# A fused attention and FP4 feed-forward kernel: rounding factors on ScalarE, scale bounds on GpSimd, joined maxima, maxima rows in two transfers, and the last batch's norms by two tiles

## What is computed

```
q_lat = einsum((x @ W_dq.T @ W_uq.T) per head, k_eff);  c_kv = x @ W_dkv.T
attn  = softmax(causal(q_lat @ c_kv.T / sqrt(hs)));     y = (attn @ c_kv) @ v_eff
x  = layernorm(x + y)
fp4(v): scale = max(max|v| over 16 / 6, 1e-12); round v/scale to {0,.5,1,1.5,2,3,4,6}; times scale
h  = silu(fp4(x) @ fp4(w_gate).T) * (fp4(x) @ fp4(w_up).T)
x  = layernorm(x + fp4(h) @ fp4(w_down).T)
```

## Time and profile before

| | |
|---|---|
| runs | 689.79, 690.15, 693.05 us; median 690.15 |
| the profiled execution | 691.02 us, its span 689.1 us |
| instructions | 15253 |
| busy, share of the span | TensorE 78%, VectorE 76%, ScalarE 60%, GpSimd 48% |
| mean granted TensorE clock | 0.912 of full |
| stages | start-up and first maxima to about 72 us; bodies of the four batches to 215, 350, 485 and 622 us; the end from 622 us |

### The profile page before, as it was taken

The page is one execution under the profiler, slowest core; times in us unless marked ns, Lnnn a source line. Parts: engine busy times, 40 slices in busy tenths (PEclk is TensorE's granted clock), DMA queues, the critical chain, the costliest instruction groups (busy, mean ns, idle before and its releaser), DMA issues.

```text
span 689.1 us, 15253 instructions
## 1 busy us (share of the span) xinstructions
PE 538.4 (78%) x5866; PEld 249.4 (36%) x5866; DVE 526.9 (76%) x920; ACT 411.3 (60%) x601; POOL 332.1 (48%) x488
## 2 busy tenths in 40 slices
PE   4356798779889899989798899898688988894523
PEld 2122343333333343434334435353233335242413
DVE  0359777768989889888888889889598894838681
ACT  2300567567777777766677777666567766674230
POOL 4440014101246766563767765537556464537262
PEclk9755699989999999999999999999999997897675
DMA  4285102922030076020130580101300000000000
GB/s 111 53 227 148 33 3 59 210 56 56 2 102 17 3 169 156 2 56 18 47 87 3 130 187 9 48 11 34 88 1 6 1 3 2 2 18 15 0 16 15
DMA packets 34797, 37.97 MB, mean 55 GB/s; under 512 B 6966, under 2 KB 20342, under 8 KB 34726
## 3 DMA queue, kind: packets, MB, share of 16 engines
q1 hardware_dynamic: 33814, 36.46, 21.9%
q10 hardware_dynamic: 912, 0.54, 0.3%
HBM read 19.64 MB, written 16.78 MB: 53 GB/s over the span
## 4 chain that ended last, share of the span: by engine, by line
PE 42%; DVE 30%; issue 8%; POOL 7%; ACT 7%; DMA 3%; SPq 2%; POOLq 0%; ACTq 0%; DVEq 0%
DVE top L924 18%; PE yt_ps L647 13%; PE ring L609 6%; PE ring L626 5%; PE misc L569 4%; PE misc L584 3%; ACT probs L804 3%; PE misc L540 2%; PE ring L596 2%; PE misc L555 1%; PE ring L569 1%; PE misc L575 1%; POOL rstd L1270 1%; DVE h_amax L1023 1%; SPq L448 1%
## 5 line engine op out<-in xcount | busy, mean ns | idle before, releaser
L924 DVE TENSOR_REDUCE top<-ring 128x2 f32<-128x1024 f32 (+3 forms) x384 | 349.2, 948 | 62.5 <-PE ring L609 31.8
L804 ACT ACTIVATE probs<-ring 128x1024 f32<-128x1024 f32 x288 | 292.8, 1026 | 111.0 <-PE ring L596 63.1
L647 PE MATMUL yt_ps<-probs,v_op 128*32 128x512 f32 (+3 forms) x1536 | 159.6, 503 | 0.4 <-ACT probs L804 0.4
L609 PE MATMUL ring<-k_op,q_op 56*128 56x512 f16 (+3 forms) x768 | 125.1, 348 | 33.0 <-DMA k_op<-scratch_k 18.1
L626 PE MATMUL ring<-q_op,k_op 59*128 59x512 bf16 (+3 forms) x768 | 120.9, 338 | 27.2 <-DVE top L924 18.8
L609 PEld LDWEIGHTS ring<-k_op,q_op 56*128 56x128 bf16 x768 | 37.9, 95 | 136.5 <-issue 105.0
L1328 POOL TENSOR_TENSOR r<-r,yq 128x128 f32<-128x128 f32 x32 | 15.0, 469 | 120.7 <-DVE yq L962 120.7
L626 PEld LDWEIGHTS ring<-q_op,k_op 59*128 59x128 f16 x768 | 37.2, 93 | 94.1 <-issue 50.1
L596 PE MATMUL ring<-ident,mask_s 64*128 64x64 bf16 x1024 | 57.6, 194 | 0.0
L596 PEld LDWEIGHTS ring<-ident,mask_s 64*128 64x128 bf16 x1024 | 46.1, 99 | 16.7 <-issue 2.4
L596 PEld LDWEIGHTS ring<-ident,mask_t 64*128 64x128 bf16 x1024 | 45.2, 97 | 15.3 <-issue 2.0
(11 more groups left out here) (183 smaller groups left out, 755.7 us busy)
## 6 DMA issues: line engine op xcount, KB each, us to landing
q_op<-scratch_q SPq DMA_DIRECT2D x32, 224.0 KB
k_op<-scratch_k SPq DMA_DIRECT2D x32, 224.0 KB
scratch_k<-k_part SPq DMA_DIRECT2D x32, 192.0 KB, 3.3
scratch_q<-q_part SPq DMA_DIRECT2D x32, 128.0 KB, 3.2
scratch_q<-q_part SPq DMA_DIRECT2D x16, 192.0 KB, 3.4
xp<-in_L_attn_x_dram SPq DMA_DIRECT2D x4, 512.0 KB, 4.4
r<-in_L_attn_x_dram SPq DMA_DIRECT2D x8, 256.0 KB, 2.9
out_dram<-z SPq DMA_DIRECT2D x8, 256.0 KB, 2.3
```

Source lines behind the costliest of these rows:

```text
L609: last = nc.tensor.matmul(ring[slot][:, e, at:at + n], q_op[lo:lo + ROWS, pair, i * P:(i + 1) * P], k_op[lo:lo + ROWS, pair, kc * CHUNK:kc ...
L647: last = nc.tensor.matmul(yt_ps[32 * q:32 * (q + 1), lo:CHUNK], v_op[:, j, 4 * a + q, :], probs[:, place[tile] % P_RING, q % 2, at:at + CH ...
L804: nc.scalar.activation(probs[:, n % P_RING, :, :], ring[(2 * n + 1) % 3][:, :, :], ACT.Exp, scale=SCALE).then_inc(t_exp.sem, 1)
L924: last = nc.vector.tensor_reduce(top[:, kc, :, p, i], ring[slot][:, :, at:at + w], AX.X, ALU.max)
```

## The change

1. *Maxima rows*: `top_parts` is laid out by row half and part, and `max_rows_in` issues two transfers of three rows each instead of six of one. SyncE, TensorE and ScalarE count two per unit.
2. *Joined maxima*: where a step has the same query tile for both head pairs (two of 18 steps), one reduction of 128x1024 elements into 128x4 replaces two of 128x512 into 128x2.
3. *Factors*: in batches 0 to 2 VectorE only masks the exponent; ScalarE makes the factor by two activations in place, `Relu(e - 1)` and `Copy(ROUND * v + ROUND)`, at new events `hmagic` and `xmagic`. `neg_one` is the bias tile, with one memset more. For the last batch VectorE makes the factor as before, at these events.
4. *Scale bounds*: in batches 0 to 2 `h_wide` is on GpSimd (new event `hwide`); the reciprocal waits for it.
5. *Last batch by two tiles*: statistics, norm, FP4 chain and transposes of x, the down sums, second norm and stores go in four parts of two tiles (k = 0 to 3) instead of two halves of four. Half 1's two parts are transposed through `yt_ps` (k = 2) and `misc` (k = 3); so are the down products. A down part waits for each tile's own copy, and for the sum of the part before it in its bank.
6. *Tile 7 of the last batch* is rounded on VectorE (`ENDING = 7`) instead of on GpSimd.
7. *Tables*: the steps of nearly all events change by 0 to 4, in the end by more; two weighings a unit move by one step each.

```diff
-    W_STEP = [4, 5, 5, 6, 10, 11, 12, 15, 16, 17, 17, 18]
+    W_STEP = [3, 5, 6, 6, 10, 11, 12, 15, 16, 17, 18, 18]
+    def part_of(b, k):
+        return (2, k // 2, slice(2 * k, 2 * k + 2)) if b == B - 1 else (PER, k, slice(PER * k, PER * (k + 1)))
 FFN:
-        "amax": [9, 17, 24, 30, 35, 40, 49, 52], "hinv": [9, 17, 24, 30, 35, 40, 49, 52],
-        "hexp": [11, 21, 26, 33, 39, 41, 51, 53], "hround": [11, 23, 27, 35, 41, 43, 52, 55], "ht": [16, 26, 29, 40, 45, 49, 58, 60],
+        "amax": [10, 15, 24, 31, 35, 41, 49, 52], "hwide": [10, 17, 25, 32, 39, 41, 49, 52],
+        "hexp": [11, 21, 26, 34, 43, 43, 50, 54], "hmagic": [12, 21, 27, 36, 44, 44, 51, 55],
+        "hround": [13, 21, 27, 36, 44, 45, 52, 55], "ht": [16, 26, 31, 40, 47, 49, 58, 62],
 TAIL tables:
-        "gate": [63, 67, 69, 75, 80, 83, 86, 90], "ht": [71, 74, 78, 80, 87, 90, 97, 97],
-        "x1t": [61, 80], "down": [86, 86, 103, 103], "lnrstd": [54, 77], "lnnorm": [55, 77], "xamax": [55, 79],
-        "amax": [67, 70, 74, 78, 82, 87, 89, 95], "hexp": [69, 72, 74, 78, 84, 87, 91, 95],
+        "gate": [64, 66, 69, 74, 81, 81, 85, 87], "ht": [73, 75, 78, 79, 90, 96, 100, 100],
+        "x1t": [63, 63, 79, 79], "down": [86, 86, 101, 101], "lnrstd": [54, 54, 76, 76], "lnnorm": [54, 54, 78, 78], "xamax": [54, 54, 79, 79],
+        "amax": [67, 70, 74, 76, 83, 84, 90, 92], "hexp": [67, 72, 74, 77, 83, 86, 90, 92],
 max_rows_in:
-                for s in range(PARTS):
-                    for e in range(2):
-                        row, m = HALF * e + ROWS + s, MX * s + PAIRS * NT * e
-                        sp.dma_start(q_op[row:row + 1, ...], top_t[m:m + PAIRS * NT, :]).then_inc(mrow_in.sem, 16)
+                for e in range(2):
+                    row, m = HALF * e + ROWS, PARTS * PAIRS * NT * e
+                    sp.dma_start(q_op[row:row + PARTS, ...], top_t[m:m + PARTS * PAIRS * NT, :]).then_inc(mrow_in.sem, 16)
 misc_job:
-                if place in last_job and not (kind == "down" and k % 2):
+                if place in last_job and not (kind == "down" and k % 2 and b < B - 1):
-                    pe.wait_ge(ht_cp.sem, ht_cp.at(b, PER * (c + 1) - 1))
+                    if b < B - 1:
+                        pe.wait_ge(ht_cp.sem, ht_cp.at(b, PER * (c + 1) - 1))
                     for n in range(half * PER // 2, (half + 1) * PER // 2):
+                        if b == B - 1:
+                            pe.wait_ge(ht_cp.sem, ht_cp.at(b, PER * c + n))
 ScalarE:
+            def factor(tile, ready, less, done, b, k):
+                act.wait_ge(ready.sem, ready.at(b, k))
+                nc.scalar.activation(tile, tile, ACT.Relu, bias=neg_one[:, :]).then_inc(less.sem, 1)
+                act.wait_ge(less.sem, less.at(b, k))
+                nc.scalar.activation(tile, tile, ACT.Copy, scale=ROUND, bias=ROUND).then_inc(done.sem, 1)
 maximum:
+                first, kc, p, at, w = S_LIST[s][0]
+                if [piece[0] for piece in S_LIST[s]] == [first, first]:
+                    both = ring[slot][:, :, 0:PAIRS * w].rearrange("q e (p n) -> q e p n", p=PAIRS)
+                    nc.vector.tensor_reduce(top[:, kc, :, :, first], both, AX.X, ALU.max).then_inc(s_max.sem, 1)
+                    return
 h_exponent (x_exponent alike):
-                dve.wait_ge(he_v.sem, he_v.at(b, t))
-                nc.vector.tensor_scalar(hc[:, n, :, :], hc[:, n, :, :], 1.0, ROUND, ALU.max, ALU.mult).then_inc(hc_v.sem, 1)
 GpSimd:
+            def h_bound(b, t):
+                n = t % 2
+                pool.wait_ge(ha_v.sem, ha_v.at(b, t))
+                nc.gpsimd.tensor_scalar(h_wide[:, n, :], h_amax[:, n, :], DOWN / 6.0, DOWN * 1e-12, ALU.mult, ALU.max).then_inc(hw_p.sem, 1)
 VectorE, last batch:
+            def end_h_round(t):
+                n, sh = t % 2, [P, FB, BLOCK]
+                dve.wait_ge(end_hc.sem, end_hc.at(0, t))
+                nc.vector.tensor_tensor(hx[:, n, :, :], hx[:, n, :, :], hc[:, n, :, :], ALU.add).then_inc(end_hu.sem, 1)
+                dve.wait_ge(end_hu.sem, end_hu.at(0, t) - ENDING)
+                nc.vector.tensor_tensor(hx[:, n, :, :], hx[:, n, :, :], hc[:, n, :, :], ALU.subtract).then_inc(end_hr.sem, 1)
+                dve.wait_ge(hs_p.sem, hs_p.at(B - 1, t))
+                dve.wait_ge(end_hr.sem, end_hr.at(0, t) - ENDING)
+                nc.vector.tensor_tensor(hx[:, n, :, :], hx[:, n, :, :], h_sc[:, n, :].unsqueeze(2).to_broadcast(sh), ALU.mult).then_inc(end_hq.sem, 1)
+            def end_sum(k):
+                dve.wait_ge(end_dn.sem, end_dn.at(0, k))
+                nc.vector.tensor_tensor(z[:, c, h, :], to[...][:, h, :], x1[:, m, :], ALU.add).then_inc(end_z.sem, 1)
```

277 lines of the change are left out of this document (171 added, 106 removed).

## The result

| | before | after |
|---|---|---|
| median of the runs | 690.15 us | 687.56 us (686.5 to 690.5) |
| ratio to before | | 0.9958, interval 0.9939 to 0.9977 |
| profiled execution | 691.0 us, span 689.1 | 687.9 us, span 686.0 |

The change takes 0.4% off, about 3 us. The forecast was 675.0 us with a range of 666 to 687: the direction was right, the size was five times too large, and the time lies outside the range.

A forecast was written before the change was run, and what follows sets the result against it. TensorE was taken to lead with VectorE close behind, and a chain after the last body. Rows 7.0, joined maxima 0.7, bodies 3.9, order 1.0 and end 2.5 made 15.1 us off 691.0, 675.9; median 675.0, range 666 to 687.

The forecast's parts named there:

- At 30% on the chain that is 2.4 us: Full bodies: 8.2 us of factors and bounds taken off VectorE, at its 30% of the chain, win 2.4 us a body.
- The trade in the bodies: Factors to ScalarE, bounds to GpSimd: net 1.3 us won in each of three bodies, 3.9 us in all.
- The rival in which ScalarE's waits take what VectorE gives: Full bodies: the moved work gains nothing, so 679 us instead of 675.0; chance 0.22.
- Rows: Maxima rows in two transfers instead of six: they land sooner and shorten four holes in TensorE, 7.0 us won.
- the first and third holes: TensorE's holes of 6.13 us before 140.51 and 4.30 us before 493.19: 1.7 and 2.7 us won by earlier rows.
- Joined maxima: 32 pairs of 512-element reductions become one of 1024 each, 2.2 to 4.8 us less on VectorE: 0.7 us won.
- Order in the last body: TensorE waits 2.6 us before transposing the last batch's first xq; transposes two steps later win 1.0 us.
- The end: Last batch's norms by two tiles: three stretches of -1.3, -1.4 and +0.2 us, 2.5 us won in all.
- The new stall at down.1: Second stretch of the end: down.1 waits for VectorE's sum of down.0, leaving VectorE idle 2.7 us.
- The third stretch: From the last down product on: half-size sum and norm save 1.1 us, a second power costs 1.3, net +0.2.
- ScalarE as the bound: Rival in the bodies: ScalarE's thirty pairs ahead of exps make the kernel slower, likely 700 us; chance 0.08.
- an even trade, no gain at the end and late rows together: Three rivals at once, in bodies, end and maxima rows: 687.4 us, within 0.5% of no change; chance 0.08.

The follow-up runs named there:

- the base: The changed kernel with factors and scale bounds of batches 0 to 2 back on VectorE, new tables kept: 680.46 us, measured again 679.60 us.

## Why the prediction was wrong, and where it was right

**What bounds the kernel: right in its rows, wrong in its use.** TensorE leads, and the limit stated was that lightening VectorE can return 6 us a body at most. The step that failed is the next one: "At 30% on the chain that is 2.4 us". It was multiplied into every microsecond taken off VectorE, and in the changed kernel TensorE's waits for `top` in a body are 6.4 us where they were 5.8 and "under 3" was forecast, with 9.6 us of VectorE's work gone. They are the same 6.4 in the base, with 5.7 us more of that work. Whether the share holds for relief alone stayed open: 25% was found, with an error twice as large as itself. With the work put elsewhere there was nothing left of it. The relief itself was mis-sized too: 8.2 us a body were forecast, and the move took 5.7 to 5.9, since at the new steps a factor takes 0.36 us and not 0.538.

**The trade in the bodies (forecast -3.9 us; it costs 7 to 9, by the ratios of the change and of the two measurements with all work back).** ScalarE's durations were right: 0.587 and 0.497 us for a tile's pair, 0.721 and 0.630 for a half batch's, against 1.09 and about 1.3. ScalarE's load by itself is worth 2.5 us, near the forecast 3.3, though not clear of nothing. What was missed is the new wait. The prediction named it, with the exp queued behind it, and then dismissed it: "The new tables put them one or two steps apart, about 2 to 4 us, which covers it mostly." The tables do not say that. Of the eight tile factors six stand one step behind their exponent, one two steps, and one at the same step; of the half batches' factors one is a step behind and the other at the same step (15); and all eight bounds stand at the step of the reciprocal that waits for them, for which VectorE stood 9.3 us. For the tiles the waits stayed small all the same (3.8 us in four of 24). For the half batches they did not: 14.3 us of idle in six instructions, 2.4 each, since VectorE was itself behind when it reached the exponent. The first half's three waits, one step apart, are as long as the second half's with none (2.4 to 2.7 and 2.1 to 2.6 us). So the count of steps alone does not tell; what tells is when VectorE gets to the exponent, and that was not looked up in the trace of before. One step more was enough: it gives back 7 us over the kernel, though the profile shows only 2.8 of them in a full body that keeps them. The rival in which ScalarE's waits take what VectorE gives was right in kind and too mild; its even trade was exceeded. The mark set for a wrong step ("over 8 us" of TensorE's wait for exps) was too coarse: the loss came about with 3.7 us. How the rest of it reached TensorE was not traced further.

On the page's rule weighed there, that relu and mul belong on VectorE (the Trainium skill, "ScalarE: Activation LUTs", "Rules for kernel authors"): it was right in sign here, as the change stands. The 9 us given as its price by engine time were mis-worked: they set ScalarE's 33.9 us against VectorE's 24.6 with the bounds among them, which went to GpSimd; for the factors alone, at the rows' durations, it is 33.9 - 15.6 = 18.3 us. That the move did cost 7 to 9 us is a coincidence: with the longest waits gone it was 1.6, which is not clear of nothing.

**Rows (forecast 7.0, measured 4.0, 2.6 to 5.5).** The issues cost 1.51 / 2 = 0.75 us, inside the bounds. The mis-sized terms are the first and third holes, 1.7 and 2.7 forecast, 0.6 and 1.0 found with the rows alone. At the first the prediction had the rows land as soon as the earlier traffic let them; their packets did move then, by 138.0, and TensorE started another 1.3 us later.

**Joined maxima (0.7).** Its duration was right, its worth nothing measurable.

**Order in the last body (1.0).** TensorE's wait there is 2.91 us instead of 2.59, so the term is wrong by its sign. Over the body's last 18 steps the changed kernel takes 34.1 us against 30.7, at a mean granted clock of 0.85 instead of 0.94; that the body is 2.3 us shorter as a whole comes from its first 54 steps. The reason was in the prediction (VectorE's chain is late), but transposes two steps later do not help when `yq` is what is late.

**The end (forecast -2.5, found -3.9).** To the first transposes of the second half, from the last exp: 22.6 us before, 20.4 after, -2.1 against -1.3. From there to the last down products 31.2 and 31.1, -0.1 against -1.4. The new stall at down.1 is there as forecast, 3.02 us against 2.7:

```profile
657.90 0.42 DVE L1151 TENSOR_TENSOR z<-misc,x 128x256 f32<-128x256 f32 x1 [3.02 <-PE misc L599]
```

What cancelled the rest is that TensorE still waits 5.60 and 4.75 us for GpSimd's rounding ahead of the last tiles' transposes. Tile 7's rounding took 0.53 us an instruction, the low value of the earlier trace rows, since GpSimd had just ended tile 6; the exclusive lock of the Trainium skill's "SBUF — State Buffer" ("SBUF: two separate sides"), weighed with 3.7 us, did not come to bear on these three, though the three ahead of them took 1.19, 0.95 and 0.83 us under GpSimd's work. The third stretch took 11.3 us instead of 13.0, -1.7 against +0.2. Its error is a missed overlap: part 2 is summed while TensorE does part 3, and the power of two elements took 0.73 us instead of 1.05.

**The range.** The case that came about was a costly trade of the bodies together with rows at 4 and a good end. The list has an even trade at 679 and ScalarE as the bound at 700, and no trade between them. It does have a place for the number: 0.08 for an even trade, no gain at the end and late rows together, 687.4. That this is within 0.2 us of the time is luck. The trade was not even but cost 7 to 9 us, the end gained 3.9, and the rows 4.

## What to carry to other kernels

Before work is moved to another in-order queue, look in the trace for when its input is ready and what stands ahead of the producer: the wait costs everything queued behind the consumer, and here one table step decided over 7 us, where the work itself left 1.6 that are not clear of nothing. Treat an engine's share of the chain as a map, not as a price: look instead at which waits for exactly that instruction would go. The cheapest gains were instructions that nobody needed yet, standing ahead of one that was awaited: moving four of them gave 9 to 11 us, by the two measurements of the version that they were moved in.

## What the runs showed of the hardware

- Issue time follows the number of transfers far more than their rows: one row 0.61 us, three rows 0.75 us of SyncE's queue.
- Fewer issues bring the next loads forward: the DMA engines' share between 138 and 139 us rose from 0.14 to 0.93. A small transfer gains from an earlier issue only as far as the loads ahead of it let it: with the last issue 2.4 us sooner, the last of the rows' packets moved 0.7 us sooner.
- VectorE's factor, the same instruction on the same 128x352 elements, takes 0.36 us at the steps of the new tables and 0.56 at those of the old.
- On GpSimd the power of 128x2 takes 0.73 us and that of 128x4 1.04: halving the elements saves 30%.
- ScalarE's pair of Relu with a bias tile and Copy takes 0.59 and 0.50 us for 352 elements a row, 0.72 and 0.63 for 512.
- Two profiles of one kernel differed by 4.4 us of span, 4.0 of it in the first and the last body.
